# Two engines' parts of a graph kernel's third edge loop: engine loops of 16 pieces in place of 1232 pieces written out

## The reference

```python
weight = jnp.einsum('rb,bio->rio', w_comp, bases)          # 32 relations from 8 bases
xw     = jnp.einsum('ni,rio->nro', h, weight)
msg    = xw[src, rel_type] * norm                          # one row of 256 per edge
out    = relu(jax.ops.segment_sum(msg, dst, num_segments=h.shape[0]))
x      = layernorm(x + out)
```

## Time and profile before

| | |
|---|---|
| median of 3 runs | 8210.89 us (8205.14 to 8220.28) |
| the profiled execution | 8210.32 us |
| its span, first to last instruction | 8208.5 us |
| share of the span busy: PE, DVE, POOL, ACT | 67%, 66%, 45%, 31% |
| mean granted TensorE clock | 0.78 |
| the third edge loop | 3766 to 5272 us, 1506 us |

### The profile page before, as it was taken

How to read it: one execution, slowest core, us unless ns; L and a number is a source line. 1 busy time by engine, 2 the same in 40 slices (tenths; PEclk the granted TensorE clock), 3 DMA queues, 4 the chain that set the end, 5 groups by cost and what they waited for, 6 DMA issues and landing times.

```text
span 8208.5 us, 116030 instructions
## 1 busy us (share of the span) xinstructions
PE 5486.4 (67%) x23622; PEld 4033.4 (49%) x23625; DVE 5435.7 (66%) x13161; ACT 2562.7 (31%) x9014; POOL 3711.2 (45%) x3988
## 2 busy tenths in 40 slices
PE   6365666526666666975555555799677777777798
PEld 4133333313433333434555555688455555555587
DVE  9767666766767664226655555675578777777666
ACT  1022222302222221112444444311345544545211
POOL 0267666536666662343555555200244444444211
PEclk8576676666667777986777777899788888888899
DMA  3232333323333331023333333355355454544411
GB/s 105 54 87 84 87 88 87 86 78 93 87 92 86 95 88 48 31 75 102 108 107 106 105 106 106 107 158 164 97 139 138 136 140 134 139 138 138 95 44 36
DMA packets 427643, 820.10 MB, mean 100 GB/s; under 512 B 75880, under 2 KB 275544, under 8 KB 426458
## 3 DMA queue, kind: packets, MB, share of 16 engines
q0 software_dynamic: 194048, 574.45, 25.2%
q1 hardware_dynamic: 230618, 231.98, 9.1%
q10 hardware_dynamic: 2304, 6.29, 0.3%
HBM read 692.86 MB, written 279.19 MB: 118 GB/s over the span
## 4 chain that ended last, share of the span: by engine, by line
PE 27%; DVE 17%; issue 10%; another core or an unknown queue 5%; SPq 3%; DMA 2%; ACT 1%; DVEq 1%; ACTq 1%; POOL 0%; POOLq 0%
PE ps L1482 4%; PE ps L1747 3%; DVE big L1417 3%; SPq L1340 2%; PE ps L1710 2%; PE ps L1936 2%; PE ps L1953 2%; DVE big L1840 2%; PE ps L831 2%; DVE big L1856 2%; DMA bas_d<-big 2%; PE ps L1432 2%; DVE big L1865 2%; DVE wreg L1828 1%
## 5 line engine op out<-in xcount | busy, mean ns | idle before, releaser
L831 PE MATMUL ps<-ring 128*128 x3528 | 1574.4, 578 | 1114.1 <-issue 478.5
L831 PEld LDWEIGHTS ps<-ring 128*128 128x128 f32 x3528 | 758.8, 266 | 1583.3 <-issue 1556.4
L1432 PE MATMUL ps<-big,ring 128*128 128x128 f32 x4928 | 885.2, 347 | 628.4 <-DVE big L1407 431.2
L745 POOL DMA_INDIRECT ring<-xl_d,idx x832 | 843.2, 1013 | 737.2 <-DVEq L640 316.3
L812 ACT CAST ring<-ohb 128x128 f32<-128x128 bf16 x1764 | 523.5, 298 | 2075.8 <-DVE ohb L775 1266.5
L1432 PEld LDWEIGHTS ps<-big,ring 128*128 128x128 f32 x4928 | 806.6, 251 | 707.0 <-DVE big L1407 486.5
L1368 POOL DMA_INDIRECT big<-x_d,idx x832 | 793.0, 953 | 790.6 <-ACT ring L1393 545.4
L1618 POOL DMA_INDIRECT ring<-kv_d,gidx x754 | 712.7, 945 | 841.5 <-issue 758.3
L745 POOL DMA_INDIRECT ring<-x_d,idx x832 | 825.9, 993 | 443.3 <-issue 225.4
L785 DVE TENSOR_TENSOR big<-big,ps 128x257 f32 (+1 forms) x1764 | 754.6, 428 | 259.1 <-issue 187.8
L1417 DVE SCALAR_TENSOR_TENSOR big<-big,ps 128x256 f32<-128x256 f32 x1232 | 590.1, 479 | 369.1 <-DMA bas_d<-big 210.1
(11 more groups left out here) (408 smaller groups left out, 9157.4 us busy)
## 6 DMA issues: line engine op xcount, KB each, us to landing
bas_d<-big SPq DMA_DIRECT2D x1232, 128.0 KB
att_d<-wreg SPq DMA_DIRECT2D x464, 132.0 KB
big<-bas_d SPq DMA_DIRECT2D x49, 1024.0 KB, 5.6
x_d<-ring SPq DMA_DIRECT2D x147, 128.0 KB, 1.7
ring<-xl_d,idx POOLq DMA_INDIRECT x832
ring<-x_d,idx POOLq DMA_INDIRECT x832
big<-x_d,idx POOLq DMA_INDIRECT x832
kv_d<-ring SPq DMA_DIRECT2D x49, 260.0 KB, 2.3
```

The costliest lines, as they stand in the source:

```text
L745: nc.gpsimd.indirect_dma_start(out=rows[:, j, :], out_offset=None, in_=table, in_offset=bass.IndirectOffsetOnAxis(ap=idx_of(c), axis=0)).t ...
L831: T.matmul(ps[k][:, 0:D], ohf[:, k, :], rows[:, slot, :].rearrange("p a d -> p (a d)"), start=True, stop=True)
L1432: last = nc.tensor.matmul(ps[j % 8][:, 0:FW].rearrange("p (n h b) -> p n h b", n=NB, h=H)[:, :, h, :], xs[:, j, h * P:(h + 1) * P], wts[:, ...
```

## The change

Two calls of `walk` lose `flat=True`, ACT's and SP's. SP's unroll goes from RING (24) to 16; the slot and the place in a group depend on `j` modulo 8 and modulo 4, which both unrolls keep. DVE, PE and POOL stand as before.

```diff
--- before.py
+++ after.py
@@ -1391,7 +1391,7 @@
                     act.wait_ge(e["arrived"], of[a] + 2 * NCK + 1)
                     act.sem_inc(s_act, 1)
                     S.copy(xs[:, j + a], rows2[:, bass.ds(of[a] % R2, 1), :].rearrange("p a d -> p (a d)")).then_inc(l2_x, 1)
-            walk(act, NCH, 16, 0, step, flat=True)
+            walk(act, NCH, 16, 0, step)
 
@@ -2112,7 +2112,7 @@
             sp.wait_ge(cf_done, 64)
             sp.dma_start(bases, A["L2_gnn_bases"].rearrange("b (h p) o -> p b h o", p=P)).then_inc(w2, 16)
             sp.wait_ge(by_rel_back, 16 * 5)
-            walk(sp, NCH, RING, FLUSH_LAG, flush_step(sp, cur, bas_d, l2_cur, NCH, 2 * NBK - 1, last2_i), flat=True)
+            walk(sp, NCH, 16, FLUSH_LAG, flush_step(sp, cur, bas_d, l2_cur, NCH, 2 * NBK - 1, last2_i))
             n2_sp(sp)
```

## The result

The kernel before takes 8208.0 us in the median of 4 runs (8202.1 to 8220.3), the changed one 8306.3 us in the median of 4 (8303.3 to 8320.7). The ratio is 1.0123, with a 95% interval of 1.0107 to 1.0139: **98 us slower**. Forecast were 163 us slower; direction, engine and stage were right, one term was too large.

What follows compares the result with a forecast made beforehand. The prediction took SP, issuing the third edge loop's stores, as full: its 1596 added instructions add 163 us to a span of 8208.5, plus 1.8 us around it, 8373 us. ACT and fetches count nothing; range 8230 to 8600 us.

Steps and rivals of the forecast that it cites:

- What bounds the kernel now: Third edge loop: no computing engine is full; SP, issuing 1232 stores and waiting 48 us in 1506, is.
- Length of the bursts: POOL's gather bursts in the third edge loop: stay 10.14 us for 12.9 pieces, since gathers per piece don't change.
- Burst price: SP during POOL's gather bursts: each instruction, added ones included, costs 0.68 us.
- Quiet price: SP in the pauses between gather bursts: one more instruction costs 0.07 us, including an estimated 30 ns gap.
- low end: SP's additions pay only 0.07 us each, 112 us, less 48 of waits and 16 of fetches: +48, 8258 us.
- DVE's wait for stores: DVE's idle before L1417 ended by a store: grows from 210 us by most of the added time.
- rival 3: SP only looks full; added instructions sink into the ring of 8 and nothing moves: 8211 us, chance 0.13.
- ACT and the fetches: ACT's 684 added instructions hide under 722 us of idling; 91 code blocks fewer on q14; both counted as nothing.
- Rival 1: Bursts keep their share of the third edge loop (0.663), not their length: +325 us, 8535 us, chance 0.15.
- Rival 2: Each of SP's 76 branches back waits for its code block, 2.2 us: 167 us on top, 8540 us, chance 0.12.
- Rival 4: SP is slow only on streamed code; held in the loop it speeds up: 8000 us, chance 0.08.
- Rival 5: The change doesn't do what it says, loops formed otherwise or same instructions: 8211 us, chance 0.02.

Runs made afterwards that it cites:

- e1: Only SP's stores run as an engine loop, ACT stays written out, against the kernel before: 8327.8 us against 8234.2, ratio 1.0125.
- e5: Kernel before, written out, with one register addition by SP ahead of each of the 1232 waits: 8299.9 us against 8234.2, ratio 1.0083.
- e8: Kernel before with three additions per store meant, folded by the build into one: 8274.9 us against 8208.8, ratio 1.0071.
- e6: Kernel before with SP reading 8 codes at once instead of 4, 154 table reads fewer: 8215.5 us against 8234.2, ratio 0.9979.
- e4b: Changed kernel without 800 of the stage's 832 gathers: 7075.5 us in one run, on the chip where the kernel before takes 7076.6.
- c1: The kernel before run once more, unchanged, on a chip of 8.2 ms: 8218.6 us in a single run, stage 1504 us.
- c2: The changed kernel run once more, against the kernel before on the same chip: 8306.4 us, ratio 1.0118, stage 1599 us.
- e2: Only ACT's shifts and copies run as an engine loop, SP stays written out, against the kernel before: 8227.6 us against 8234.2, ratio 0.9995.

## Why the prediction was right, and where it was off

**What bounds the kernel now: right.** SP was named full by 48 us of waiting in 1506 although its medians promised 419 us of work. e1 (+94 us by the medians), e5 and e8 (+66 both) and e6 (-17) all move the time through SP's instructions alone, and e4b shows no loss where SP isn't full.

**Instruction counts: right.** 1140 additions on L1339 of 33 ns (forecast 37), 76 branches more of 45 ns at the median, 5599 - 4005 = 1594 instructions more (forecast 1596).

**Length of the bursts: right.** The prediction kept 10.14 us of burst for 12.9 pieces, 999 us in all. The 792 gathers make 996 us in c1 and in c2, and the slow steps stay within them. They come in more and shorter lots, since 111 intervals between gathers are over 1.6 us in c1 and 140 in c2. That alone costs and saves nothing: e2 has 120 such intervals, and its slow steps last 974 us beside c1's 970.

**What a burst lets through: this is the term that was mis-sized.** The words were "Burst price: 0.68 us" for an added instruction, and "in it SP manages 15 / 4.56 = 3.3 stores instead of 4.6". By that the bursts of the stage should have lost 28% of their stores, and these should have gone to the pauses. Measured, they lost 2% in c2 (452 to 442; 8% in the pair of the result, 453 to 418). SP gets through 20.7 instructions in 10.14 us of burst where it had 15.2. So what was taken for a price of each instruction is a number of slow steps in a given time, and added instructions mostly pass between them. With 4.5 stores in the burst instead of 3.3, the prediction's own sum has 8.4 for the quiet part at 0.71 us, 6.0 us: +0.8 us a cycle, some +80 us, beside +95 in the stage. Why the slow steps come at this rate, and why those of 1.4 us became fewer (283 to 243), the runs don't show.

**Quiet price: a little low.** 0.07 us was an estimate; the additions of L1339 take 0.085 us from their start to the next start in c2's pauses. A branch takes 45 ns, but the next instruction starts 0.27 us after it at the median.

The quick heap grew by 166 us, close to the forecast's 163, but that is chance: the heap also holds the quick steps inside the bursts, and the pauses themselves grew by 95. The measured time fell into the prediction's range by its low end, additions that pay the quiet price alone, less 48 and 16 us. That case was nearer to what happened than the one that was taken, except that a third of the additions cost nothing and SP's waits covered little.

**SP's own waits.** Forecast was that they fall below 48 us; they are 36.1 us, and from c1 to c2 they go from 45.5 to 40.6. They absorbed 12 and 5 us, not the up to 48 of the low bound.

**DVE's wait for stores: half right.** "Grows from 210 by most of the added time" undersold it: it grew by 240 us with 98 us added. The "remote" waits went from 235 us to 28.8 + 11.5 = 40, 195 us less, and DVE's other idling grew by 51, which leaves the +97. That is the overlap which rival 3 pointed to, and e6 shows its other side.

**ACT and the fetches: right.** e2 is at 0.9995, and 88 blocks went.

**The rivals.** Rival 1 (the burst keeps its share, 8535 us) is refuted: the bursts stay at 996 us while the stage grows, 0.66 of it before and 0.62 after. Rival 2 (the head is fetched again, 8540 us): 57 blocks came on q14 in the stage, 145 before; there are no 76 new ones, and none of SP's branches has its next instruction over 1.5 us later. The Trainium skill (Runtime: NRT & Kernel Launch, Instruction fetch mechanics) lets a taken branch stall only where its target is outside the blocks held; with bodies of 73 and 109 instructions it never did here, or at no price that e2 shows. Rival 3 (SP only looks full and nothing moves) is refuted by e1, e5 and e8. Rival 4 (the price is paid for streamed code) is refuted: SP's instructions held in the loop still take up to 740 ns, and additions written out cost no more than those of the loop (e5: 0.055 us each; the change: 98 / 1596 = 0.061). Rival 5 falls with the rows of L1339 and L95, which show the loop.

## What to carry to other kernels

- An engine that only issues DMAs can be the full one without a busy number to show for it. The sign is how little it waits for those it serves; compare its median durations with its maxima in the stage, and price an added instruction at what it costs this engine, here 0.06 us for a register addition of 33 ns.
- A mean step in a slow stretch, time by instructions, isn't yet the price of one more instruction. The slow steps can go by time: here their number stayed within 5% while the instructions beside them rose by a third. An addition then costs only where the engine is quick. Sort by place, burst and pause, before and after a probe such as e5, rather than by length of step alone.
- A named wait is not a gain to be had. 240 us of new store waits cost 98 us, and 93 us fewer brought 17, since another wait stands right behind.

## What the runs showed that was not expected

- On chips where the kernel takes 8.2 ms the queues of SP and ACT take steps of 0.7 or 1.4 us during POOL's gathers, whatever the instruction: SP's moves of 29 ns up to 1432 ns, ACT's branch of 45 ns up to 730. DVE's queue doesn't: the register operation ahead of each L1407 takes 69 to 75 ns every time. On one other chip the same program takes 7076.6 us, 14% less, and the longest move with all gathers running is 45 ns. Runs must be compared on one chip only. What makes the chips differ is open, and so is what makes the steps slow.
- Handing half of the stores to ACT made the kernel slower by 2% on either kind of chip, though SP was the full engine on the 8.2 ms one.
- The build folds successive constant additions to a register into one.
